# Differential attention rewritten as a pipeline over its iterations, with halved maxima and no filler matmuls

## The chip, the cores and the metric

The program runs on one core of a Trainium2 chip. A core has a matrix engine (TensorE; PE in the tables, its weight loads PEld), VectorE (DVE), ScalarE (ACT), GpSimd (POOL) and SyncE (SP), which issues the transfers. The engines run their own instruction lists and wait for each other by semaphores. The metric is device time in microseconds (us) of one execution, the median of several runs. TensorE's granted clock is given as a share of 2.4 GHz: 1.00 is full speed, 0.50 is 1.2 GHz.

## The reference, cut to what matters

The whole program is a GRU over 4 sequences of 512 steps, differential attention on its states, a spectral filter with the output projection, a second attention and a layer of experts. Only the differential attention is touched:

```
q = rotary(query @ Wq);  k = rotary(query @ Wk)      # 32 half heads of 16 numbers
v = query @ Wv                                       # 16 heads of 2 * 16
s = einsum('bthd,bshd->bhts', q, k) * scale
s = where(causal mask, s, -1e30);  a = softmax(s, axis=-1)
o1 = einsum('bhts,bshd->bthd', a, v1);  o2 = ... v2  # once for q1,k1 and once for q2,k2
attn1 - lambda_full * attn2, filtered along the sequence
```

Each head has two maps of scores (q1 k1 and q2 k2), both weigh the same v, and the difference of the results goes on.

## The kernel before, in words

`diff_attention_stage` works in 16 iterations: 4 sequences times 4 groups of 4 heads. One iteration holds 4 heads of 32 numbers on 128 partitions; each head has a block of 32 partitions, and map a of it (a = 0 or 1) uses 16 of them. All numbers are fp32 unless said otherwise. PSUM is one tensor `da_ps` of 8 banks of 512 numbers. An iteration of the kernel before has these parts, one after another on TensorE:

- Projection (`project`, L633 to L649): keys and queries, 4 matmuls of 128x512 each (L640); ScalarE copies them out (L687); a matmul that swaps the pairs of the rotary embedding (L644); VectorE and GpSimd form the rotated values `rot`; then 16 matmuls of 128x128 for v (L647). VectorE writes the keys of map 0 into `kp` and ScalarE those of map 1 (L691), each with the other map's rows as zeros. q is `rot` as it is.
- Output of the finished iteration (`output`): 4 transposes (L662) and 4 filler matmuls.
- Maximum part (L454 to L469): for each of the 4 blocks of 128 queries, the longest first, and each map, four score matmuls, one for each head (L464), 4 mask matmuls in bf16 (L468), and one VectorE reduction over the 4 heads (L544). Two sets of 4 banks take turns; a block of index i has (i+1)*128 keys.
- Maxima to rows: VectorE rounds the maxima to bf16 and keeps the rest as a second column of `spread` (L547 to L550); 8 transposes (L477) turn them into rows; ScalarE and VectorE copy these to `top` in bf16 (L520, L554). 3 filler matmuls before and 5 behind the transposes.
- Key part (L480 to L510), 8 groups (4 blocks of keys times 2 maps), each in halves of two heads: 2 score matmuls with keys on the partitions (L494), 2 bf16 matmuls that subtract the maximum (minus one times `top`, L497), 2 mask matmuls (L501); ScalarE takes the exponential of the half (L530); VectorE adds the exponentials up in `total` (L559, L563); 4 matmuls weigh v (L508), one group behind the scores.
- Sums (L514): 8 matmuls that sum `total` over the partitions. Then ScalarE forms a reciprocal by Ln and Exp, VectorE refines it (L567, L569) and scales and combines the maps (L747, L750). This runs on while TensorE projects the next iteration.

The filler matmuls (`keep_warm`, L446 to L449) multiply zeros into a free bank and nothing reads them; 12 stand in an iteration. The order of the work is written out by hand; semaphores carry the waits. SyncE loads the states `hb` and weights `wg` of the next iteration when v is done.

The second attention, `full_attention_stage` (names `fa_`, lines L930 to L1288), is not changed. It is already a pipeline over iterations: it works on the maximum part of iteration `it` and puts the projections of `it + 1` between the pieces, takes maxima in halves of two heads, and has no filler. It has no mask and a single map. Its rows are therefore of use here.

Of the kernel before, what the change touches and what calls it, by code (L numbers as in the profile page):

```python
# [407 lines left out]
class AttentionCore:  # L408
# [3 lines left out]
    def __init__(self, nc, ctx, sem, prefix, NA, scale, causal):  # L412
        self.nc, self.NA, self.scale, self.causal = nc, NA, scale, causal

        def sb(name, shape, dt=F32):
            return ctx.enter_context(nc.sbuf_tensor(prefix + name, shape, dt))

        self.probT = sb("probT", [P, 2, HG, T])
        self.mx, self.mxb = sb("mx", [P, TT, NA, HG]), sb("mxb", [P, TT, NA, HG], BF16)
        self.spread = sb("spread", [P, TT, NA, HG, DH])  # L420
        self.kp = sb("kp", [P, NA, T])
        self.negone, self.top = sb("negone", [P, P], BF16), sb("top", [P, NA, T], BF16)
        self.ones, self.rec = sb("ones", [P, P]), sb("rec", [P, NA, T])
        self.err, self.total = sb("err", [P, NA, T]), sb("total", [P, NA, HG, T])
        self.warm = sb("warm", [P, T], BF16)
        self.added, self.summed_up = sem("added"), sem("summed_up")

        self.ps = ctx.enter_context(nc.psum_tensor(prefix + "ps", [P, 8, T], F32))
        self.core_set, self.scored, self.max_done, self.spread_done = (sem(n) for n in ("core_set", "scored", "max_done", "spread_done"))
        self.max_cols, self.top_act, self.top_dve, self.rounded = sem("max_cols"), sem("top_act"), sem("top_dve"), sem("rounded")  # L430
        self.keys_scored, self.exp_done, self.refined, self.banks_free = (sem(n) for n in ("keys_scored", "exp_done", "refined", "banks_free"))
        self.product, self.ln_done, self.rec_done = sem("product"), sem("ln_done_core"), sem("rec_done")
        self.SET = 3
        self.groups = [(i, a) for i in range(TT) for a in range(NA)]

        self.queries = [(i, a) for i in reversed(range(TT)) for a in range(NA)]

    def setup(self, dve):
        nc = self.nc
        nc.vector.memset(self.warm[:], 0.0)  # L440
        nc.vector.memset(self.ones[:], 1.0).then_inc(self.core_set, 1)
        nc.vector.memset(self.negone[:], -1.0).then_inc(self.core_set, 1)
        nc.vector.memset(self.spread[:], 0.0).then_inc(self.core_set, 1)
        dve.wait_ge(self.core_set, self.SET)

    def keep_warm(self, bank, n):  # L446

        for _ in range(n):
            self.nc.tensor.matmul(self.ps[:, bank, :], self.warm[:, 0:P], self.warm[:], start=True, stop=True)  # L449

    def tensor(self, pe, it, v, q, ident, identb, mask, maskT):
        nc, NA, NG = self.nc, self.NA, len(self.groups)
        slots = [slice(DH * h, DH * h + DH) for h in range(HG)]
        for m, (i, a) in enumerate(self.queries):  # L454
            L = (i + 1) * P if self.causal else T
            bank = 4 * (m % 2)
            if m == 1:

                pe.wait_ge(self.banks_free, it * 1 + 1)
            if m >= 2:  # L460

                pe.wait_ge(self.max_done, it * NG + m - 1)
# [3 lines left out]
            if self.causal:  # L466
                for h in range(HG):
                    last = nc.tensor.matmul(self.ps[:, bank + h, i * P:L], identb, mask, start=False, stop=True)  # L468
# [1422 lines left out]
```

## Time and profile before

| | |
|---|---|
| median of 3 runs | 4769.63 us (4766.91 to 4773.21) |
| profiled execution, its own time | 4766.31 us |
| span of the profiled execution | 4764.7 us |
| TensorE busy | 3911.8 us, 82% |
| VectorE, ScalarE, GpSimd busy | 2238.0, 1304.5, 382.9 us |
| mean granted TensorE clock | 0.94 |

The span runs from the first to the last instruction; 1.6 us of the execution's time lie around it. Busy times add up the instructions of an engine. TensorE's are partly models: of matmuls that overlap, their starts are reliable and their durations overlap. An fp32 matmul shows as two records, so that four matmuls are "x8". In a timeline, the bracket behind an instruction is the idle time of the engine before it and what ended that. The differential attention runs from 2137.4 us to 3023.7 us.

### The profile page before, as it was taken

What the parts mean: (1) busy time and instruction counts of PE and PEld (TensorE: products, weight loads), DVE (VectorE), ACT (ScalarE), POOL (GpSimd) and SP (SyncE); (2) the same over time, 40 slices, a digit from 0 to 9 for tenths busy, and PEclk for the clock granted to TensorE, in tenths of its full rate; (3) what the DMA queues carried; (4) which work ended last, traced back from release to release, by engine and by line L of the source; (5) the groups of instructions that cost most, each with busy time, mean ns of one, the idle gap of its engine ahead of it and who ended that gap; (6) DMA issues with size and microseconds to landing.
All of it is one profiled execution on the core that took longest, in us unless ns stands there. A gap on an engine that the chain in (4) does not pass through costs nothing. (4 is left out here: it accounts for less than half of the span.)

```text
span 4764.7 us, 168106 instructions
## 1 busy us (share of the span) xinstructions
PE 3911.8 (82%) x69376; PEld 2562.6 (54%) x69376; DVE 2238.0 (47%) x6160; ACT 1304.5 (27%) x4110; POOL 382.9 (8%) x829
## 2 busy tenths in 40 slices
PE   8788888888888888879999999576999979488830
PEld 4377777777777777764444444333333334244410
DVE  2155555555555555545555555233666633221224
ACT  1033333333333333322223333122444411011100
POOL 0000000000000000000000000000000004300034
PEclk9999999999999999999999999788999979799975
DMA  2230000000000000000100000201111111287866
GB/s 67 48 147 0 0 0 0 0 0 0 0 0 0 0 0 0 0 22 31 46 31 31 31 31 31 74 18 42 60 62 46 46 49 67 90 258 240 256 175 157
DMA packets 144600, 256.56 MB, mean 54 GB/s; under 512 B 25943, under 2 KB 76375, under 8 KB 142516
## 3 DMA queue, kind: packets, MB, share of 16 engines
q1 hardware_dynamic: 118516, 201.96, 13.1%
q0 software_dynamic: 21248, 53.30, 4.0%
q10 hardware_dynamic: 4800, 0.81, 0.1%
q8 instruction: 23, 0.38, 0.0%
q14 instruction: 13, 0.11, 0.0%
HBM read 147.95 MB, written 62.92 MB: 44 GB/s over the span
## 5 line engine op out<-in xcount | busy, mean ns | idle before, releaser
L305 PE MATMUL gru_pr<-gru_whh,h 128*4 128x128 f32 x16384 | 544.4, 274 | 229.8 <-DVE h L396 229.8
L305 PEld LDWEIGHTS gru_pr<-gru_whh,h 128*4 128x4 f32 x16384 | 388.9, 87 | 373.3 <-DVE h L396 367.1
L305 PE MATMUL gru_pz<-gru_whh,h 128*4 128x128 f32 x16384 | 541.7, 273 | 2.3 <-issue 2.3
L305 PE MATMUL gru_pn<-gru_whh,h 128*32 128x128 f32 x16384 | 541.6, 273 | 0.0
L305 PEld LDWEIGHTS gru_pn<-gru_whh,h 128*32 128x32 f32 x16384 | 458.4, 110 | 1.3
L305 PEld LDWEIGHTS gru_pz<-gru_whh,h 128*4 128x4 f32 x16384 | 438.9, 87 | 9.9 <-issue 2.4
L376 DVE STREAM_TRANSPOSE gru_tr<-gru_pr 128x128 f32<-128x128 f32 x512 | 162.2, 317 | 379.7 <-PE gru_pr L305 379.7
L340 ACT ACTIVATE gru_rn<-gru_pre 128x16 f32<-128x16 f32 x512 | 118.5, 231 | 706.9 <-DVE gru_pre L378 706.9
L389 DVE STREAM_TRANSPOSE gru_tz<-gru_pz 128x64 f32<-128x64 f32 x1024 | 194.8, 228 | 121.3 <-PE gru_pz L305 121.3
L530 ACT ACTIVATE da_probT<-da_ps 128x1024 f32<-128x1024 f32 (+3 forms) x256 | 180.1, 703 | 195.4 <-PE da_ps L501 194.1
L280 POOL COPY gru_pick<-ident 128x4 f32 x512 | 95.9, 187 | 1687.5 <-PE gru_pz L296 1682.2
L296 PE MATMUL gru_pz<-gru_zin,gru_pick 128*4 128x128 f32 x4096 | 206.3, 273 | 19.6 <-DMA gru_whh<-in_L_cond_W_hh 19.6
L396 DVE TENSOR_TENSOR_SCAN h<-gru_d 128x32 f32<-128x32 f32 x1024 | 185.8, 223 | 77.8 <-ACT gru_d L345 76.3
L380 DVE STREAM_TRANSPOSE gru_tn<-gru_pn 128x128 f32<-128x128 f32 x512 | 162.2, 317 | 119.6 <-PE gru_pn L305 119.6
L544 DVE TENSOR_REDUCE da_mx<-da_ps 128x4 f32<-128x2048 f32 (+3 forms) x128 | 184.0, 1486 | 70.8 <-PE da_ps L468 70.5
L345 ACT ACTIVATE gru_d<-gru_tz 128x8 f32<-128x8 f32 x1024 | 177.3, 216 | 128.9 <-DVE gru_tz L389 128.9
L342 ACT ACTIVATE gru_d<-gru_narg 128x32 f32<-128x32 f32 x512 | 120.8, 236 | 329.6 <-DVE gru_narg L385 329.6
L494 PE MATMUL da_ps<-da_rot,da_kp 32*128 32x128 f32 (+3 forms) x1024 | 206.9, 480 | 0.0
L290 PE MATMUL gru_pn<-gru_bias,gru_one 128*32 128x128 f32 x4096 | 206.4, 273 | 0.0
L1620 PE MATMUL ex_pg<-ex_wg,ex_xT 128*128 128x384 f32 x512 | 192.6, 523 | 0.0
L1436 POOL DMA_INDIRECT xg<-ro_yb,ro_slot x96 | 96.4, 1004 | 1058.4 <-DVE ro_slot L1545 1030.3
L1222 DVE TENSOR_REDUCE fa_mx<-fa_ps 128x2 f32<-128x1024 f32 x128 | 150.6, 1218 | 53.8 <-PE fa_ps L1042 53.7
(270 smaller groups left out, 5521.7 us busy)
## 6 DMA issues: line engine op xcount, KB each, us to landing
ex_wg<-in_L_ffn_gate_up_proj SPq DMA_DIRECT2D x64, 768.0 KB, 5.3
ex_wd<-in_L_ffn_down_proj SPq DMA_DIRECT2D x64, 384.0 KB, 6.1
xg<-gru_zeros SPq DMA_DIRECT2D x4, 4096.0 KB
da_hb<-wide SPq DMA_DIRECT2D x16, 1024.0 KB, 4.7
fa_hb<-xnT SPq DMA_DIRECT2D x16, 1024.0 KB
ex_xg<-xg SPq DMA_DIRECT2D x64, 256.0 KB, 2.7
eo<-ex_eo POOLq DMA_DIRECT2D x64, 256.0 KB, 6.3
da_wg<-ahead SPq DMA_DIRECT2D x48, 256.0 KB, 4.8
```

The source lines that it names most:

```text
L290: nc.tensor.matmul(pn[32 * j:32 * j + 32, 0:P], one[:], bias[:, j, :], start=True, stop=False)
L296: last = nc.tensor.matmul(pz[32 * j:32 * j + B, par, 0:P], pick[:, par, :], zin[:, j * P:(j + 1) * P], start=True, stop=False)
L305: last = nc.tensor.matmul(rows(j), of(c), whh[:, c, g, j, :], start=(c == 0 and start), stop=(c == KD - 1))
L345: nc.scalar.activation(cb(d1[:, half * HS:(half + 1) * HS, 2]), tz[:, half * HC:(half + 1) * HC, 0:B], ACT.Sigmoid).then_inc(z_act, 1)
L376: nc.vector.transpose(tr[:].rearrange("p c x -> p (c x)"), pr[:, 0:P]).then_inc(tr_done, 1)
L380: nc.vector.transpose(tn[:], pn[:, 0:P]).then_inc(tn_done, 1)
L389: nc.vector.transpose(tz[:, half * HC:(half + 1) * HC, :].rearrange("p c x -> p (c x)"), pz[:, par, half * 64:(half + 1) * 64]).then_inc(t ...
L396: nc.vector.tensor_tensor_scan(t.h[:].rearrange("p c x -> p (c x)")[:, half * 64:(half + 1) * 64:2], d0[:, of, :].rearrange("p c o -> p (c ...
L494: nc.tensor.matmul(self.ps[:, h, q0:T], self.kp[slots[h], a, kt * P:(kt + 1) * P], q[slots[h], q0:T], start=True, stop=False)
L530: nc.scalar.activation(self.probT[:, n % 2, heads, q0:T], self.ps[:, heads, q0:T], ACT.Exp, scale=self.scale).then_inc(self.exp_done, 1)
L544: nc.vector.tensor_reduce(self.mx[:, i, a, :], self.ps[:, bank:bank + HG, 0:L], AX, ALU.max).then_inc(self.max_done, 1)
L1620: last = nc.tensor.matmul(pg[:, u % 2, 0:2 * I], xT[:, u % 2, k, :], wg[:, u, k, :], start=(k == 0), stop=(k == KD - 1))
```

## The change

The stage is written anew as one function; `AttentionCore` is gone. The reference's result is computed as before. What is different:

- Iteration `it` now holds the maximum part and the key part of `it`, with the projections of `it + 1` and the sums and the output of `it - 1` between the pieces. The first and the last iteration are written out apart.
- The maximum part takes 16 pieces of two heads (`score_for_max`, m = 0 to 15) in place of 8 of four heads. Pieces take banks 0, 1 and 2, 3 in turn.
- q gets a copy for each map, made by ScalarE, with the other map's rows zero. In `kp` of each map one of these unused rows holds minus one. The maxima, transposed in fp32, are added to q by VectorE (`maxima_into_q`), so that the score matmul itself subtracts the maximum. The matmuls with `top`, its two copies and the rounding to bf16 are gone.
- v passes through a second buffer `vn`, the weighed sums are copied to `pv` by ScalarE before they are scaled.
- There is no filler matmul.

```
-    def keep_warm(self, bank, n):
-        for _ in range(n):
-            self.nc.tensor.matmul(self.ps[:, bank, :], self.warm[:, 0:P], self.warm[:], start=True, stop=True)
-                    for h in heads:
-                        last = nc.tensor.matmul(self.ps[:, h, q0:T], self.negone[slots[h], :], self.top[slots[h], a, q0:T],
-                                                start=False, stop=not self.causal)
...
-        "half": np.stack([p % DH < DQ, p % DH >= DQ], 1).astype(f),
+        "half": np.stack([p % DH < DQ, p % DH >= DQ, -(p % DH == DQ).astype(f), -(p % DH == 0).astype(f)], 1).astype(f),
...
 TensorE
+    def score_for_max(it, m):
+        i, a = queries[m // 2]
+        L = (i + 1) * P
+        heads = (2 * (m % 2), 2 * (m % 2) + 1)
+        if m in (0, 2):
+            pe.wait_ge(q_ready, it * 2 + (a + 1))
+            pe.wait_ge(keys_ready, it * 2 + (a + 1))
+        if m >= 2:
+            pe.wait_ge(max_done, it * HV + (m - 1))
+        for h in heads:
+            nc.tensor.matmul(ps[:, h, 0:L], q[slots[h], a, i * P:(i + 1) * P], kp[slots[h], a, 0:L], start=True, stop=False)
+        for h in heads:
+            last = nc.tensor.matmul(ps[:, h, i * P:L], identb[:], maskb[:], start=False, stop=True)
+        last.then_inc(scored, 1)
+    def iteration(it, first=False, last=False):
+        j = it + 1
+        def maxima(m):
+            score_for_max(it, m)
+            score_for_max(it, m + 1)
+        maxima(0)
+        if not first:
+            sum_exponentials(it - 1)
+        maxima(2)
+        if not last:
+            project(j, 1, (0, 1), first)
+        maxima(4)
+        if not last:
+            project(j, 1, (2, 3))
+        maxima(6)
+        if not last:
+            project(j, 0, (0, 1), first)
+        maxima(8)
+        if not last:
+            project(j, 0, (2, 3))
+            swap_pairs(j, 1)
+        maxima(10)
+        if not first:
+            output(it - 1)
+        maxima(12)
+        maxima(14)
+        if not last:
+            swap_pairs(j, 0)
+        maxima_to_rows(it, first)
+        for n in range(NG):
+            score_keys(it, n)
+            if n < TT and not last:
+                if n == 0:
+                    pe.wait_ge(q_topped, it * 2 + 1)
+                project_v(j, n)
+            if n == 1:
+                pe.wait_ge(v_set, it * 1 + 1)
+                if not last:
+                    pe.wait_ge(sined, j * 2 + 2)
+                else:
+                    pe.wait_ge(pv_kept, it * 1)
+            if n:
+                weigh_values(it, n - 1)
+        weigh_values(it, NG - 1)
...
 ScalarE
+    def halves_of_q(j):
+        act.wait_ge(rotated, j * 2 + 3)
+        for a in range(2):
+            nc.scalar.activation(q[:, a, :], rot[:, 0, :], ACT.Copy, scale=half[:, a:a + 1]).then_inc(q_ready, 1)
+    def iteration(it, first=False, last=False):
+        j = it + 1
+        if not first:
+            move_v(it)
+            reciprocal(it - 1)
+        if not last:
+            keep_raw(j, 1)
+            keep_raw(j, 0)
+        if not first:
+            keep_output(it - 1)
+        for n in range(NG):
+            if n == 0 and not first:
+                act.wait_ge(added, it * NG)
+            exponentials(it, n)
+            if n == TT and not last:
+                keep_v(j)
+        if not last:
+            act.wait_ge(keys_scored, it * HV + HV)
+            halves_of_q(j)
+        keep_products(it, first)
...
 VectorE
+    def output(it):
+        dve.wait_ge(rec_done, it * 1 + 1)
+        nc.vector.tensor_tensor(err[:], ps[:, BSUM:BSUM + 2, :], rec[:], ALU.mult).then_inc(refined, 1)
+        dve.wait_ge(refined, it * 2 + 1)
+        nc.vector.scalar_tensor_tensor(rec[:], err[:], -2.0, rec[:], op0=ALU.add, op1=ALU.mult).then_inc(refined, 1)
+        dve.wait_ge(refined, it * 2 + 2)
+        dve.wait_ge(pv_kept, it * 1 + 1)
+        for a, o in enumerate((o1, o2)):
+            nc.vector.scalar_tensor_tensor(o[:], pv[:, a, :], -1.0, rec[:, a, :], op0=ALU.mult, op1=ALU.mult).then_inc(scaled, 1)
+        dve.wait_ge(scaled, it * 2 + 2)
+        nc.vector.scalar_tensor_tensor(aT[:], o2[:], nlam[:, 1:2], o1[:], op0=ALU.mult, op1=ALU.add).then_inc(aT_ready, 1)
+    def maxima_spread(it):
+        dve.wait_ge(max_done, it * HV + HV)
+        for a, col in enumerate((DQ, 0)):
+            nc.vector.tensor_copy(spread[:, :, a, :, col], mx[:, :, a, :]).then_inc(spread_done, 1)
+    def maxima_into_q(it):
+        for a in range(2):
+            dve.wait_ge(max_cols, it * 2 + (a + 1))
+            nc.vector.tensor_tensor(q[:, a, :], q[:, a, :], ps[:, BSUM + a, :], ALU.add).then_inc(q_topped, 1)
+    def iteration(it, first=False, last=False):
+        j = it + 1
+        for m in range(4):
+            maximum(it, m)
+        if not first:
+            output(it - 1)
+        for m in range(4, 14):
+            maximum(it, m)
+        if not last:
+            times_sine(j, 1)
+        maximum(it, 14)
+        maximum(it, 15)
+        maxima_spread(it)
+        if not last:
+            times_sine(j, 0)
+        maxima_into_q(it)
+        for n in range(NG):
+            if n == 3 and not last:
+                rotate(j, 1)
+                rotate(j, 0)
+            if n == NG - 1 and not last:
+                dve.wait_ge(keys_scored, it * HV + HV)
+                halves_of_keys(j)
+            accumulate(it, n)
```

The order of instructions on TensorE shows the interleaving. In the kernel before the loop's maximum part starts like this, each row a run of equal matmuls with L464 the scores and L468 the masks:

```order
L464 MATMUL da_ps<-da_kp,da_rot 128x512 x4
L468 MATMUL da_ps<-da_maskb,da_identb 128x128 x4
L464 MATMUL da_ps<-da_kp,da_rot 128x512 x4
L468 MATMUL da_ps<-da_maskb,da_identb 128x128 x4
L462 ISA
L464 MATMUL da_ps<-da_kp,da_rot 128x384 x4
```

In the changed kernel the same place in the loop, with L528 the scores, L530 the masks and L503 projections of the next iteration, reads:

```order
L503 MATMUL da_ps<-da_hb,da_wg 128x512 x2
L526 REGISTER_ALU
L528 MATMUL da_ps<-da_kp,da_q 128x384 x2
L530 MATMUL da_ps<-da_maskb,da_identb 128x128 x2
L526 REGISTER_ALU
L528 MATMUL da_ps<-da_kp,da_q 128x384 x2
L530 MATMUL da_ps<-da_maskb,da_identb 128x128 x2
L503 MATMUL da_ps<-da_hb,da_wg 128x512 x2
```

Two of the eight projection matmuls now stand between every two pairs of pieces, and a piece is two heads. On VectorE the last iteration, whose rows are not broken by register instructions, shows where the output of the iteration before has gone. L763 are the maxima, L767 to L775 the output, L780 `spread`, L785 the maxima into q:

```order
L763 TENSOR_REDUCE da_mx<-da_ps 128x2 x4
L767 TENSOR_TENSOR da_err<-da_ps,da_rec 128x1024
L769 SCALAR_TENSOR_TENSOR da_rec<-da_err,da_rec 128x1024
L773 SCALAR_TENSOR_TENSOR da_o<-da_pv,da_rec 128x512 x2
L775 SCALAR_TENSOR_TENSOR da_aT<-da_o,da_nlam 128x512
L763 TENSOR_REDUCE da_mx<-da_ps 128x2 x12
L780 COPY da_spread<-da_mx 128x4x4 x2
L785 TENSOR_TENSOR da_q<-da_q,da_ps 128x512 x2
```

The output, which stood behind all additions of its own iteration, is now queued behind the fourth maximum of the next, and twelve maxima are queued behind it.

## Rows read from the trace of the kernel before

**Rows 1.** Timeline of GpSimd: start, duration, engine, line; one L628 pair an iteration.
```profile
2144.07 1.26 POOL L628 TENSOR_TENSOR da_cc<-da_qk,da_cs 128x512 f32<-128x512 f32 x1 [31.36 <-ACT da_qk L687]
...
2309.64 1.48 POOL L628 TENSOR_TENSOR da_cc<-da_qk,da_cs 128x512 f32<-128x512 f32 x1 [49.75 <-ACT da_qk L687]
...
2364.09 1.48 POOL L628 TENSOR_TENSOR da_cc<-da_qk,da_cs 128x512 f32<-128x512 f32 x1 [49.75 <-ACT da_qk L687]
...
2965.03 1.48 POOL L628 TENSOR_TENSOR da_cc<-da_qk,da_cs 128x512 f32<-128x512 f32 x1 [49.75 <-ACT da_qk L687]
```
**Rows 2.** Timeline of TensorE, one iteration at full clock, parts before its maximum part.
```profile
2521.93 1.90 PE L514 MATMUL da_ps<-da_total,da_ones 128*32 128x512 f32 x16
2523.76 7.13 PE L640 MATMUL da_ps<-da_hb,da_wg 128*128 128x512 f32 x16
2530.74 1.98 PE L644 MATMUL da_ps<-da_qk,da_swap 128*128 128x512 f32 x4
2532.55 3.73 PE L647 MATMUL da_ps<-da_wg,da_hb 128*128 128x128 f32 x32
2536.12 0.60 PE L662 MATMUL da_ps<-ident,da_aT 128*128 128x128 f32 x4
```
**Rows 3.** Timeline of TensorE's weight loads, the same iteration: starts of the parts.
```profile
2537.51 0.31 PEld L464 LDWEIGHTS da_ps<-da_kp,da_rot 32*128 32x128 f32 x8 [0.42 <-issue]
...
2553.43 0.30 PEld L494 LDWEIGHTS da_ps<-da_rot,da_kp 32*128 32x128 f32 x4 [0.42 <-issue]
...
2576.28 0.24 PEld L514 LDWEIGHTS da_ps<-da_total,da_ones 128*32 128x32 f32 x8
```
**Rows 4.** Timeline of TensorE, the same iteration: halves of 512 and of 128.
```profile
2553.43 1.13 PE L494 MATMUL da_ps<-da_rot,da_kp 32*128 32x512 f32 x4
2554.40 0.38 PE L497 MATMUL da_ps<-da_top,da_negone 32*128 32x512 bf16 x2
2554.71 0.29 PE L501 MATMUL da_ps<-da_maskTb,da_identb 128*128 128x128 bf16 x2
2554.93 1.13 PE L494 MATMUL da_ps<-da_rot,da_kp 32*128 32x512 f32 x4
...
2574.21 0.49 PE L494 MATMUL da_ps<-da_rot,da_kp 32*128 32x128 f32 x4
2574.54 0.22 PE L497 MATMUL da_ps<-da_top,da_negone 32*128 32x128 bf16 x2
2574.69 0.29 PE L501 MATMUL da_ps<-da_maskTb,da_identb 128*128 128x128 bf16 x2
```
**Rows 5.** Groups by line and shape: busy, mean ns of one, idle before.
```profile
L544 DVE TENSOR_REDUCE da_mx<-da_ps 128x4 f32<-128x1024 f32 x32 | 39.1, 1221 | 2.0 <-PE da_ps L468 1.8
L544 DVE TENSOR_REDUCE da_mx<-da_ps 128x4 f32<-128x512 f32 x32 | 22.0, 687 | 6.1 <-PE da_ps L468 6.0
L735 DVE TENSOR_TENSOR da_sw<-da_ps,da_cs 128x512 f32<-128x512 f32 x32 | 21.9, 685 | 31.8 <-PE da_ps L644 31.8
L691 ACT ACTIVATE da_kp<-da_rot,da_half 128x512 f32<-128x512 f32 x16 | 11.6, 722 | 30.8 <-DVE da_rot L738 30.8
```
**Rows 6.** Timeline of TensorE in the second attention: a projection in two pieces, the output wait.
```profile
3573.45 1.98 PE L1004 MATMUL fa_ps<-fa_hb,fa_wg 128*128 128x512 f32 x4
...
3575.37 1.14 PE L1042 MATMUL fa_ps<-fa_kp,fa_q 32*128 32x512 f32 x8
...
3581.31 1.10 PE L1020 MATMUL fa_ps<-fa_sq,fa_headones 128*128 128x512 f32 x2 [1.23 <-DVE A L1242]
```
**Rows 7.** Stretches: length, busy time of PE, PEld, DVE, ACT, POOL, then granted clock.
```profile
3512.50:3517.50 5.00, 3.77 (x8) 1.51 (x5) 3.54 (x4) 1.22 (x2) 0.00 (x0) 0.67 0.00 0
...
3811.00:3829.00 18.00, 12.58 (x52) 4.18 (x56) 8.08 (x10) 4.47 (x5) 0.00 (x0) 0.53 0.00 0
```
**Rows 8.** Timeline of VectorE: the output at the stage's end.
```profile
3017.34 1.23 DVE L567 TENSOR_TENSOR da_err<-da_ps,da_rec 128x1024 f32<-128x1024 f32 x1 [3.68 <-ACT da_rec L536]
...
3021.19 0.75 DVE L750 SCALAR_TENSOR_TENSOR da_aT<-da_o,da_nlam 128x512 f32<-128x512 f32 x1
```

More of the change, by code:

```diff
@@ L658, in output, with sum_exponentials @@
+            def sum_exponentials(it):
+                for a in range(2):
+                    pe.wait_ge(added, it * NG + (NG - 1 + a))
+                    for h, sl in enumerate(slots):
+                        last = nc.tensor.matmul(ps[sl, BSUM + a, :], ones[:], total[:, a, h, :], start=True, stop=True)
+                last.then_inc(summed_up, 1)
             def output(it):
@@ L661, in output @@
                 for i in range(TT):
[L662 removed]
+                    last = nc.tensor.transpose(ps[:, BOUT, i * P:(i + 1) * P], aT[:, i * P:(i + 1) * P], t.ident[:])
                 last.then_inc(a_psum, 1)
[L664 to L673 removed]
@@ L674, in _, with maxima_to_rows @@
-            attend(NIT - 1)
+            def maxima_to_rows(it, first):
+                pe.wait_ge(spread_done, it * 2 + 2)
+                for a in range(2):
+                    if a == 1 and not first:
+                        pe.wait_ge(a_written, it * 1)
+                    for i in range(TT):
+                        last = nc.tensor.transpose(ps[:, BSUM + a, i * P:(i + 1) * P],
+                                                   spread[:, i, a, :, :].rearrange("p h d -> p (h d)"), t.ident[:])
+                    last.then_inc(max_cols, 1)
@@ L675, in _ @@
+            project(0, 1, range(KD), first=True)
+            project(0, 0, range(KD), first=True)
+            swap_pairs(0, 1)
+            swap_pairs(0, 0)
+            for tt in range(TT):
+                project_v(0, tt)
+            over_iterations(pe, iteration)
+            sum_exponentials(NIT - 1)
             output(NIT - 1)
@@ L709, in _, with exponentials @@
-            core.scalar(act, NIT - 1)
-            output(NIT - 1)
+                                     ps[:, BOUT, :].rearrange("p (i f) -> p i f", f=P), ACT.Copy).then_inc(a_written, 1)
+            def exponentials(it, n):
+                kt, a = groups[n]
+                q0 = kt * P
+                if n >= 2:
+                    act.wait_ge(product, it * NG + (n - 1))
+                    act.wait_ge(added, it * NG + (n - 1))
+                for half_of in range(2):
+                    heads = slice(2 * half_of, 2 * half_of + 2)
+                    act.wait_ge(keys_scored, it * HV + (2 * n + half_of + 1))
+                    nc.scalar.activation(probT[:, n % 2, heads, q0:T], ps[:, heads, q0:T], ACT.Exp, scale=scale).then_inc(exp_done, 1)
```

375 lines of the change are left out of this document (153 added, 222 removed).

## The prediction, made before the changed kernel ran

> **What bounds the kernel now.** I first read the slices and group table of the page to place the stage, then the timelines. GpSimd's line 628 runs twice an iteration and serves as a clock [rows 1]: the reader is to see its idle bracket repeat, 49.75 us, and to measure start to start. At full clock an iteration takes 2364.09 - 2309.64 = 54.45 us. From the first iteration's mark to the sixteenth's there are 820.96 us, 15 x 54.45 would be 816.75, so stretches at the low clock cost 4.2 us in all.
>
> The TensorE timelines cut such an iteration [rows 2, 3]; what counts is the distance between starts: sums 1.83, the two projections 6.98, two swaps 1.81, v 3.57, output and filler 1.4, from the maximum part to the key part 15.92, key part 22.85. They add up to the iteration: everything is in series on TensorE. Yet it is not all TensorE's work. In the 15.92 us it waits for VectorE's maxima and then for the turn from maxima to rows; the other parts are dense. The change can gain there, and in the matmuls that subtract the maximum, and it can lose by giving TensorE more or smaller work. So I write TensorE's list of the new iteration with prices from these rows and look for waits.
>
> **Prices.** In the key part a half of two heads has its scores, then `top`, then the mask [rows 4]. At length 512 scores take 0.97, `top` 0.31, masks 0.22; at 128 scores take 0.33 and `top` 0.15. Lengths between lie on the line (scores 0.76 and 0.54, `top` 0.25 and 0.20). A half without `top` is then 1.19, 0.98, 0.76 and 0.55 for 512, 384, 256 and 128. That two heads and their mask cost this in the new maximum part too is an assumption: the same shapes, the other operand as weights. A maximum over two heads reads half as much: 1.22 us for 1024 numbers, 0.69 for 512 [rows 5], by the same line 0.95 for 768 and 0.42 for 256.
>
> Projections are now cut in pieces of two matmuls among 32-row scores. The second attention does that: such a piece takes 1.92 us from start to start [rows 6], against 6.98 / 4 = 1.75 in one run [rows 2]. I charge 0.17 for each cut, for the four pieces of v too. The Trainium skill, "TensorEngine Tiling (Array Packing)", Tiling Modes, says that changing the tiling mode drains the engine, which speaks against cutting and halving. The trace agrees, with these 0.17 us; without a drain the eight pieces would be 1.4 us cheaper an iteration.
>
> **The new iteration, maximum part.** TensorE's work in it: pieces 4 x (1.19 + 0.98 + 0.76 + 0.55) = 13.9; sums of the iteration before 1.85; four pieces of projection 4 x 1.92 = 7.7; one swap 0.9; output 0.5. Together 24.85. Halving costs TensorE here (four heads ran side by side before, now two), but VectorE was the limit there, and the projections fill what would be idle.
>
> The wait in it: VectorE's output (L767 to L775) is 4.6 us long, as at the stage's end [rows 8], and stands behind the fourth maximum. The fourth piece ends at 2.38 + 1.85 + 2.38 = 6.6 us, its maximum at 8.0, the output at 12.6, the fifth maximum at 13.6. Behind the output on VectorE stand all later maxima, and the seventh piece needs the fifth maximum. TensorE has only a piece of projection, two pieces of maxima and another piece of projection until then: 6.6 + 1.92 + 1.96 + 1.92 = 12.4. It waits some 1.2 to 1.3 us; the second attention shows the like, 1.23 us on its output [rows 6]. The reciprocal on ScalarE is no wait: it is two activations of 1024 numbers behind the sums, about 1 us each by L691's 0.72 for 512, and ends near 6.5, before VectorE comes to it. Later VectorE catches up, since it has 0.4 to 0.7 us of work to a piece.
>
> So the last piece ends at 26.1. Behind it VectorE still has a sine product (0.69) and two maxima (0.42 each), partly begun, and is done 1.0 later; two small copies 0.35, four transposes 0.7, maxima into q of map 0, 0.69 (priced by L735, [rows 5]), hand-overs 0.1. The second swap and the second sine lie beside these. Key part at 26.1 + 2.85 = 29.0.
>
> **Key part.** It was 22.85 [rows 3]. The 16 `top` pairs go: 4 x (0.31 + 0.25 + 0.20 + 0.15) = 3.65. v comes in: 3.57 + 4 x 0.17 = 4.25. ScalarE's exponentials hide behind TensorE as before, for its halves still last longer than an exponential, and v lies between. VectorE's two rotations and two multiplies for the keys, under 1 us each as L735 is, fit: it waits between its additions for exponentials. At the end the next maxima need q of map 0, which ScalarE writes after the last exponential: 0.72 [rows 5], beside 0.3 of weighing v. That wait is 0.45. Sum 22.85 - 3.65 + 4.25 + 0.45 = 23.9.
>
> The full-clock iteration is 29.0 + 23.9 = 52.9 us, 1.6 less than before (52.85 unrounded). SyncE's loads, now released when v ends about 8 us before the iteration's end (four short groups and the end), have some 15 us until their first use, the fifth piece of the next maximum part; if that cover were gone, TensorE would wait for the rest of the transfer in every iteration.
>
> **The ends.** The first iteration lacks sums, output and their wait: 52.85 - 1.85 - 0.5 - 1.3 = 49.2, 5.25 less than an old one. Fourteen run at 52.85: 14 x 1.6 = 22.4 less. The last has no projections to put under VectorE: output done at 12.6, then twelve maxima that take turns with their pieces, about 9.1, then 1.85 to the key part, at 23.55; key part 19.2 without v and without the wait. Together 42.75 to the last sums, where before it were 15.92 + 22.85 = 38.8: 4.0 more. The start pays 1.3 (a second copy of v and a half of q in ScalarE's list before the first piece, about as long as L691's 0.72 each [rows 5]). Sum of these: -5.25 - 22.4 + 4.0 + 1.3 = -22.35.
>
> **The clock.** The profile shows full clock, 2.4 GHz, in most of the stage. In the second attention, without filler, a stretch around the output wait fell to 0.67 in the mean, that is partly to 1.2 GHz, and 18 us of the last iteration, where TensorE waited for maxima, ran at 0.53 [rows 7]. The Trainium skill, "TensorE: Matmul & The Clock Gate", Part 1, says that the throttled state is the default and that activity releases it; the trace agrees, with those 0.53. By that the filler's absence counts against the change. I take 1 for the first iteration, 5 for the middle ones (about what the 15 iterations of before lost, 4.2 [rows 1], since the waits are now shorter but fewer are filled), and 7 for the last: 18 us at 0.53 with TensorE busy 12.6 of them lose up to 6 to 7. That makes 13 in place of 4.2, 8.8 more.
>
> **Sum.** -22.35 + 8.8 = -13.5 against the profiled execution's 4766.31: 4752.8. The median of the runs shown is 3.3 above the profiled one, so 4756 us.
>
> **Bounds.** Mode changes: 1.4 us less an iteration if the cuts cost nothing, 1.5 more if each of the 16 new pieces pays 0.1 more than its half did. Output wait: 0 to 2.5 (double, if the ends of the hand-overs come late). The end of the maximum part: at best 1.85, as in the last iteration; at worst the 3.6 of before. The copies from PSUM to SBUF and back (pv, vn, v) lie on ScalarE, busy a third of the iteration: 0, and if they delayed the reciprocal they would move the output by at most 1 us. Minus one as a row of keys adds no instruction: 0, but the second `half` multiply has an added term, 0 to 0.1. Together an iteration lies between 51.2 and 54.3, that is -23 to +20 around the sum; the clock adds -7 to +20.
>
> **Rivals.**
> - *The clock falls at the output wait of every iteration.* Place: the seventh piece. For it: the second attention fell there [rows 7]. Against: it has the same wait in all its iterations and fell in few. At about 1.7 us each (a 5 us stretch at 0.67), 14 cost 24 in place of 5: 4756 + 19 = 4775, no change.
> - *Long low stretches without filler, slower.* The same place, but the clock stays low over the rest of the maximum part, some 12 us in which TensorE is now dense, so that each loses up to 6. With 10 of 14 iterations: 60 - 5 = 55 more, 4811. It decides from about 5 such iterations on. For it: 18 us in one piece in the last iteration of the second attention. Against: only where TensorE had long waits again and again, here they are 1.3, 0.5 and 0.45 in 53 us.
> - *Small pieces eat the gain.* TensorE is the bound all through, and every cost of switching shows. At 53.8 an iteration: 14 x 0.95 = 13 more, 4769, no change.
> - *Hand-overs cost less than I charge.* No output wait in excess and cheap cuts, 51.4 an iteration: 20 less, 4736.
>
> **Chances.** Forecast 0.50 (its own range 4743 to 4768), clock at every wait 0.14, long low stretches 0.12, small pieces 0.11, cheap hand-overs 0.13. A measurement tells 0.2% of this kernel from no change, which is 9.5 us: below 4760 is faster, above 4779 slower. Faster: four fifths of the forecast's 0.50, the 0.13 and 0.02 of the others, 0.55. Slower: 0.12 and 0.03 of the others, 0.15. Same: 0.30. The range that leaves out two tenths: 4732 to 4784.
>
> **What would show it.** In the new profile: GpSimd's mark near 52.9 us apart at full clock; the seventh piece waiting about 1.3 us for a maximum behind VectorE's output; 2.4 to 3.4 us between the last piece and the key part, partly filled by a swap; key part near 23.9 to the next piece, with 0.45 of it a wait for ScalarE's q; the last iteration's maximum part near 23.5, at a clock near 0.5 for much of it. Wrong it is if pieces of two heads take more than 1.3 us at 512, if projection pieces take more than 2, if VectorE is late at other pieces, or if low stretches stand in most iterations.

## The result, and the profile after

The kernel became slower: 4807.5 us in the median (4795.6 to 4819.5, 7 runs) against 4769.6 us (4762.4 to 4787.6, 7 runs), a ratio of 1.0078 with an interval of 1.0059 to 1.0098. The forecast was 4756 us, with a range up to 4784: the sign was wrong and the time lies outside the range. The profiled execution took 4803.15 us (span 4801.5). The page shows more TensorE time in fewer matmul records (68,672 instead of 69,376), and a lower clock above all in the 26th of its 40 slices, which holds the end of the stage (5 tenths, 7 before):

```profile
PE 3973.3 (83%) x68672; PEld 2565.5 (53%) x68672; DVE 2265.1 (47%) x6302; ACT 1324.4 (28%) x4142; POOL 379.3 (8%) x829
...
PEclk9999999999999999999999999588999989799965
```

I measure the stage from the start of its first projection to the end of its last sums, both on TensorE's timeline: 877.8 us before, 909.1 after, so 31.4 of the 37 us are there. GpSimd's mark (first of each pair, L489 now) answers to [rows 1]:

```profile
2166.84 1.26 POOL L489 TENSOR_TENSOR da_cc<-da_qk,da_cs 128x512 f32<-128x512 f32 x1 [21.76 <-ACT da_qk L647]
...
2385.63 1.26 POOL L489 TENSOR_TENSOR da_cc<-da_qk,da_cs 128x512 f32<-128x512 f32 x1 [44.27 <-ACT da_qk L647]
...
2439.56 1.26 POOL L489 TENSOR_TENSOR da_cc<-da_qk,da_cs 128x512 f32<-128x512 f32 x1 [44.27 <-ACT da_qk L647]
...
2495.22 1.26 POOL L489 TENSOR_TENSOR da_cc<-da_qk,da_cs 128x512 f32<-128x512 f32 x1 [44.31 <-ACT da_qk L647]
...
2931.62 1.26 POOL L489 TENSOR_TENSOR da_cc<-da_qk,da_cs 128x512 f32<-128x512 f32 x1 [44.27 <-ACT da_qk L647]
```

From the second row to the third it is 53.93 us, an iteration at full clock (54.45 before, 52.85 forecast). To the fourth it is 55.66: 6 of the 14 middle iterations are so long. All fourteen take 764.8 us. TensorE's timeline shows the cause (line, shape of weights and data, then the wait ahead):

```profile
2435.88 0.92 PE L528 MATMUL da_ps<-da_kp,da_q 32*128 32x384 f32 x4
2436.73 0.28 PE L530 MATMUL da_ps<-da_maskb,da_identb 128*128 128x128 bf16 x2
2436.85 1.94 PE L503 MATMUL da_ps<-da_hb,da_wg 128*128 128x512 f32 x4
2439.80 0.92 PE L528 MATMUL da_ps<-da_kp,da_q 32*128 32x384 f32 x4 [1.02 <-DVE da_mx L763]
2440.87 0.91 PE L528 MATMUL da_ps<-da_kp,da_q 32*128 32x384 f32 x4
2441.72 0.39 PE L530 MATMUL da_ps<-da_maskb,da_identb 128*128 128x128 bf16 x2
2441.89 3.57 PE L503 MATMUL da_ps<-da_hb,da_wg 128*128 128x512 f32 x4
```

The seventh piece waits 1.02 us for VectorE, which is busy with the output. Right behind that wait the projection piece takes 3.57 us instead of 1.94: half clock, 1.65 us lost. The last iteration is far worse. It takes 68.0 us from its first piece (2972.07) to its last sums (3040.07), where the old one took 38.9 and the forecast said 49.75. The clock falls near 2981.1, inside the sixth piece, while TensorE is at work: the scores take 1.05 us instead of 0.92 and the mask behind them 0.39 instead of 0.29. The wait of 4.00 us for the seventh piece comes behind that:

```profile
2979.14 0.91 PE L528 MATMUL da_ps<-da_kp,da_q 32*128 32x384 f32 x4
2979.98 0.29 PE L530 MATMUL da_ps<-da_maskb,da_identb 128*128 128x128 bf16 x2
2980.41 1.05 PE L528 MATMUL da_ps<-da_kp,da_q 32*128 32x384 f32 x4
2981.39 0.39 PE L530 MATMUL da_ps<-da_maskb,da_identb 128*128 128x128 bf16 x2
2985.79 1.65 PE L528 MATMUL da_ps<-da_kp,da_q 32*128 32x384 f32 x4 [4.00 <-DVE da_mx L763]
```

In the stretches (length, busy time of PE, PEld, DVE, ACT, POOL, granted clock, DMA) it doesn't come back before the last sums, though from the start of the key part (3003.37) on TensorE is busy without a gap:

```profile
2975.00:2980.00 5.00, 4.96 (x33) 1.40 (x26) 3.04 (x3) 2.08 (x2) 0.00 (x0) 1.00 0.02 3
...
3010.00:3040.00 30.00, 30.00 (x146) 10.13 (x148) 8.69 (x8) 9.21 (x14) 0.00 (x0) 0.50 0.00 1
```

The kernel before went through the same iteration at full clock, though TensorE was idle for a quarter of its maximum part and nothing full-width but the short masks stood between its pieces. Its own projections and v stood right ahead of them, and its pieces held four heads. It entered its key part high, with filler of 3 and 5 matmuls (L449) around the turn, which the change takes out:

```profile
2974.00:2989.00 15.00, 10.96 (x108) 5.33 (x107) 11.89 (x11) 0.69 (x2) 0.00 (x0) 1.00 0.01 1
2989.00:3013.00 24.00, 23.88 (x194) 9.49 (x192) 9.83 (x9) 11.73 (x17) 0.00 (x0) 1.00 0.00 1
```

### The profile page after: what moved, and what is told of

Its sections match the earlier page's. It is cut to its first block and busy times, and to the rows that moved or that the text cites. A ratio compares the mean times of both kernels' runs of the same rounds, so it can differ in the third digit from the quotient of the medians.

```text
span 4801.5 us, 166900 instructions
## 1 busy us (share of the span) xinstructions
PE 3973.3 (83%) x68672; PEld 2565.5 (53%) x68672; DVE 2265.1 (47%) x6302; ACT 1324.4 (28%) x4142; POOL 379.3 (8%) x829
## 5 line engine op out<-in xcount | busy, mean ns | idle before, releaser
L763 DVE TENSOR_REDUCE da_mx<-da_ps 128x2 f32<-128x1024 f32 (+3 forms) x256 | 208.2, 823 | 160.2 <-PE da_ps L530 157.4
L528 PE MATMUL da_ps<-da_kp,da_q 32*128 32x128 f32 (+3 forms) x1024 | 215.5, 498 | 23.4 <-DVE da_mx L763 18.3
L566 PE MATMUL da_ps<-da_q,da_kp 32*128 32x128 f32 (+3 forms) x1024 | 217.3, 502 | 5.4 <-DVE da_q L785 5.4
```

Source lines behind the costliest of these rows:

```text
L528: nc.tensor.matmul(ps[:, h, 0:L], q[slots[h], a, i * P:(i + 1) * P], kp[slots[h], a, 0:L], start=True, stop=False)
L566: nc.tensor.matmul(ps[:, h, q0:T], kp[slots[h], a, kt * P:(kt + 1) * P], q[slots[h], a, q0:T], start=True, stop=False)
L763: nc.vector.tensor_reduce(mx[:, i, a, banks], ps[:, banks, 0:(i + 1) * P], AX, ALU.max).then_inc(max_done, 1)
```

## The experiments

All start from the changed kernel. "Stage" is measured as above, "last" from the last iteration's first piece to its last sums, both in the profiled execution. A clean iteration is the shortest of the fourteen middle ones; it is at full clock in all runs but e6_nomask, where every one of them has a low stretch. The ratio is to the kernel before on the same chip; a run of one execution has none. The stages can be compared from chip to chip: the changed kernel's took 909.1 us on one and 909.5 on another.

| run | clean iteration | last | stage | ratio (interval) |
|---|---|---|---|---|
| before | 54.45 | 38.9 | 877.8 | 1 |
| after | 53.93 | 68.0 | 909.1 | 1.0078 (1.0059 to 1.0098) |
| e12_after_again | 53.93 | 68.0 | 909.5 | 1.0088 (1.0066 to 1.011) |
| e1_last_fill | 53.93 | 66.4 | 907.9 | 1.0061 (1.0035 to 1.0086) |
| e4_split_out | 52.84 | 65.9 | 881.5 | 1.0011 (0.9993 to 1.0029) |
| e5_pairs | 52.55 | 66.4 | 900.0 | one execution |
| e6_nomask | 53.57 | 61.5 | 897.1 | one execution |
| e7_pairs_split | 52.05 | 64.3 | 867.9 | 0.9993 (0.9965 to 1.002) |
| e8_dense_last | 53.93 | 54.7 | 894.4 | one execution |
| e2_key_fill | 53.93 | 56.1 | 893.5 | one execution |
| e9_top_last | 55.01 | 58.6 | 908.7 | one execution |
| e10_split_fill | 52.84 | 47.7 | 861.5 | 0.9984 (0.9964 to 1.0004) |
| e11_all | 52.05 | 47.4 | 852.5 | 0.9969 (0.9953 to 0.9986) |

**e1_last_fill: filler once in the last iteration.**

```
+                if last:
+                    pe.wait_ge(pv_kept, it * 1)
+                    keep_warm(5, 18)      # behind the sixth piece; matmuls of 128x512 bf16 on zeros
```

> The changed kernel with 18 filler matmuls (128x512, bf16, zeros) in the last iteration alone, behind its sixth piece, where TensorE waited 4.0 us for the seventh maximum. The last iteration, first piece to last sums, took 68.0 us in the changed kernel. My theory: that one wait brought the clock down to 1.2 GHz and the thin pieces of two heads behind it did not bring it back; with the wait filled the last iteration takes 43 to 47 us and the kernel about 22 less than the changed one (4785). Rival: the last iteration falls by itself, because no full-width matmuls of projections stand in it; then the clock falls later in it and it still takes 55 to 68 us. A second rival, that the filler only delays: 68 or more.

The clock had fallen inside the sixth piece here too, 0.9 us ahead of the filler. The filler covered the wait and brought the clock back up, and it stayed up for 4 us of thin pieces behind it. Then it fell, with no wait near (the fall is inside a piece at 2996.3), and stayed down:

```profile
2991.80:2996.80 5.00, 4.86 (x30) 1.99 (x28) 2.99 (x4) 0.00 (x0) 0.00 (x0) 0.97 0.00 0
2996.80:3001.80 5.00, 5.00 (x28) 2.74 (x24) 2.06 (x4) 0.60 (x1) 0.00 (x0) 0.50 0.00 0
...
3006.80:3040.00 33.20, 33.20 (x133) 10.09 (x132) 9.14 (x8) 10.49 (x14) 0.00 (x0) 0.50 0.00 1
```

The last iteration gained 1.6 us and took 66.4, within the 55 to 68 of the first rival. My theory of that moment, that the one wait is what costs, fell; covering it is not enough.

**e4_split_out: VectorE's output in two stretches.**

```
-                for m in range(4, 14):
+                for m in range(4, 6):
                     maximum(it, m)
+                if not first:
+                    output_rest(it - 1)   # the two o and aT; err and rec stay behind the fourth maximum
+                for m in range(6, 14):
+                    maximum(it, m)
```

> The changed kernel with VectorE's output cut in two: the two refining operations stay behind the fourth maximum, the three that scale and combine stand behind the sixth. Theory: the wait of 1.02 us before the seventh piece goes in each of the 14 middle iterations, and with it the fall of the clock that stood behind it in 6 of 14 (1.65 us each): an iteration at full clock takes 52.9 in place of 53.93, mean 53.0 in place of 54.63, the kernel about 22 less (4785). Rival: the wait only moves to the ninth piece or to the end of the maximum part, where VectorE is late by as much; the iteration stays at 53.9.

Confirmed for the middle iterations. The seventh piece no longer waits and the next projection piece (2330.53) runs at full clock:

```profile
2326.64 1.94 PE L503 MATMUL da_ps<-da_hb,da_wg 128*128 128x512 f32 x4
2328.50 0.91 PE L528 MATMUL da_ps<-da_kp,da_q 32*128 32x384 f32 x4
2329.35 0.28 PE L530 MATMUL da_ps<-da_maskb,da_identb 128*128 128x128 bf16 x2
2329.56 0.92 PE L528 MATMUL da_ps<-da_kp,da_q 32*128 32x384 f32 x4
```

All fourteen iterations take 52.8 to 52.9 us. That is 1.09 us less each, the wait itself, and no 1.65 for the clock in any. So in the middle iterations the wait was what lowered the clock; why it did so in only 6 of 14 was not tested. The stage is 27.6 us shorter, nearly all that the change had lost. The last iteration is nearly as bad as ever, 65.9 us: the wait in it came down to 2.13 us, and the clock fell all the same, 0.1 us behind its end.

**e5_pairs and e6_nomask: is it the pieces of two heads?** The first puts the scores of four heads ahead of their masks, still in two signals (the edit below is shortened); the second has no masks there.

```
-                for h in heads:                                     # e5: four heads, then their masks
+                for half_of in range(2):
+                    if m >= 2: pe.wait_ge(max_done, it * HV + (m + half_of - 1))
+                    for h in (2 * half_of, 2 * half_of + 1): scores
+                for half_of in range(2): masks of its two heads, then_inc(scored, 1)
```

> The changed kernel with the two pieces of one query block and map issued together: scores of all four heads, then the masks of both halves, each half still signalled apart. Theory: a piece of two heads pays for two of four row groups and for one change to the full array and back, so the pair at 512 falls from 2.55 us to about 1.4 and TensorE's work in the maximum part falls by some 8 us; but the scores of a pair now wait for both maxima before, and the wait behind VectorE's output grows to about 3 us, so the iteration at full clock is 53.0 to 53.6 and the clock falls there more often. Rival: the price of halving is small, the pair takes over 2 us, and the longer waits make the iteration 55 or more.

> The changed kernel without the 32 mask matmuls of the maximum part; the maxima then run over all keys up to the block's end, later ones too. Theory: the full-array masks between 32-row scores are what keeps two pieces from running side by side; without them two pieces at 512 take 1.1 to 1.3 us from the first's start to the end of issue of the second in place of 2.55, and VectorE bounds the maximum part: iteration about 49 us. Rival: only the masks' own 0.22 us go, two pieces take 2.1, the iteration 50.5 to 51.

Four heads with masks take 1.40 us at length 512 (two pieces took 2.55), without masks 1.07. TensorE does become shorter, but VectorE does not, and the wait grows by what TensorE saved: 2.36 us in e5_pairs, 3.51 in e6_nomask, and the projection behind it is at half clock in 11 of 14 middle iterations of the one and in all 14 of the other:

```profile
2335.99 1.78 PE L528 MATMUL da_ps<-da_kp,da_q 32*128 32x384 f32 x8 [2.36 <-DVE da_mx L763]
2337.70 0.40 PE L531 MATMUL da_ps<-da_maskb,da_identb 128*128 128x128 bf16 x4
2337.93 3.62 PE L503 MATMUL da_ps<-da_hb,da_wg 128*128 128x512 f32 x4
```

```profile
2434.74 2.52 PE L528 MATMUL da_ps<-da_kp,da_q 32*128 32x384 f32 x8 [3.51 <-DVE da_mx L761]
2437.18 3.78 PE L503 MATMUL da_ps<-da_hb,da_wg 128*128 128x512 f32 x4
```

Cheaper pieces alone are worth little, 9.1 us of the stage in e5_pairs: VectorE's output is the limit there. Both expectations had the price of a pair right and the iteration wrong: 52.55 instead of 53.0 to 53.6 us in e5_pairs, with more low clock, and 53.6 to 55 instead of 49 in e6_nomask.

**e7_pairs_split: both.** The edits of e5_pairs and e4_split_out together.

> The scores of four heads and then their masks, in two signals (as in e5_pairs), together with VectorE's output in two stretches (as in e4_split_out). Theory: a piece of four heads then costs 0.1 us or more less than two pieces, and with the split no wait stands before the seventh piece, so the clock doesn't fall: a clean iteration of about 50.5 to 51.5 us against 52.85 in e4_split_out and 53.93 of the changed kernel; fourteen iterations give 28 to 30 us less than e4_split_out, so about 0.995 of the kernel before. The last iteration stays at half clock, about 65 us. Rival: TensorE isn't the bound of the maximum part once its pieces are short, VectorE's maxima are; then the waits come at other pieces, the clock falls there, and an iteration stays at 52.5 to 54 us.

The stage gains another 13.6 us on e4_split_out, but the fourteen middle iterations only 6.3 of the 28 to 30 that I expected of them; 4.8 come from the first iteration and 1.6 from the last. Clean iterations take 52.05 us, and 5 of the 14 take 52.9 to 53.2 because the clock dips. The rival holds for the missing part: the seventh piece still waits 0.24 us for VectorE's maxima, and four later ones 0.78, 0.16, 0.23 and 0.40.

**e8_dense_last: full-width filler between all pieces of the last iteration.**

```
+                if last: keep_warm(5, 8)     # in place of each projection piece: 8, 8, 8 and 12
+                if last: keep_warm(5, 4)     # in place of the swap before maxima_to_rows
+                    if n < TT and last: keep_warm(BV, 4)   # in place of each v piece
```

> The changed kernel, with 8, 8, 8, 12 and 4 filler matmuls of 128x512 bf16 on zeros in the last iteration where the other iterations have their projections and transposes, and 4 at each place of a v piece; their results are read by nobody. Theory: what holds the clock in the other iterations is the full-width work that stands between the thin pieces; with it the last iteration runs at full clock for nearly all of its length and takes 52 to 55 us from its first piece to its last sums, filler included, against 68.0 us without. Rival: the clock falls at the first wait of 4 us for the output of the iteration before and stays low whatever stands between; then 75 us or more.

Confirmed: 54.7 us, one dip, and back to full clock behind it, where in the changed kernel it never came back:

```profile
2975.00:2988.00 13.00, 12.01 (x68) 4.00 (x64) 10.10 (x11) 3.48 (x4) 0.00 (x0) 1.00 0.00 1
2988.00:2993.00 5.00, 4.88 (x18) 1.79 (x19) 2.85 (x4) 0.00 (x0) 0.00 (x0) 0.67 0.00 0
2993.00:3010.00 17.00, 16.66 (x103) 7.93 (x103) 7.23 (x13) 2.94 (x4) 0.00 (x0) 1.00 0.01 1
```

Some 13 us of useless matmuls made the iteration 13 us shorter. They also fill most of the wait, of which 1.11 us are left; that the wait isn't the cause rests on e1_last_fill and on where the clock falls.

**e2_key_fill and e9_top_last: does the key part need `top` to hold the clock?**

```
+                    keep_warm(5, 16)         # both: last iteration, ahead of the key part
+                    if last:                 # e9: between scores and masks
+                        for h in heads:
+                            nc.tensor.matmul(ps[:, h, q0:T], warm[slots[h], 0:P], warm[slots[h], q0:T], start=False, stop=False)
```

> The changed kernel with 16 filler matmuls of 128x512 ahead of the key part of the last iteration, and nothing else. Theory: the clock rises to 2.4 GHz with the filler and falls back to half in the midst of the key part, as it did after the filler of e1_last_fill, so that from the end of the filler to the last sums there are 28 us or more. Rival: entered at full clock, the key part holds it, as in the kernel before, and takes 21 to 24 us.

> The changed kernel, in the last iteration alone: 16 filler matmuls ahead of the key part, and in the key part a bf16 matmul of 32 rows of zeros for each head between its scores and its mask, as the row of the maximum stood there in the kernel before. Theory: the kernel before kept full clock through its last key part because its three thin matmuls to a head kept TensorE busier; the key part then stays at 2.4 GHz after the filler and takes 21 to 24 us. Rival: the two kernels differ there only by the state in which they enter the key part; then e9_top_last and e2_key_fill do the same, whichever that is.

The rival of both holds. Entered at full clock, the key part keeps it without `top`; it takes 20.8 us (3009.87 to 3030.71) instead of 36.7 in the changed kernel. With `top` it takes 22.9 and keeps it too. In e2_key_fill:

```profile
2985.00:3005.00 20.00, 15.88 (x69) 8.06 (x70) 10.68 (x18) 0.60 (x1) 0.00 (x0) 0.50 0.00 0
3005.00:3010.00 5.00, 5.00 (x23) 2.44 (x23) 1.38 (x2) 0.00 (x0) 0.00 (x0) 0.81 0.00 0
3010.00:3030.00 20.00, 20.00 (x148) 7.53 (x152) 9.12 (x7) 10.87 (x15) 0.00 (x0) 1.00 0.01 2
```

So the same list of matmuls, without a gap, takes 36.7 us at 1.2 GHz or 20.8 us at 2.4 GHz, by the level at which it was entered. The other runs bear this out. The last key part was entered low and took 36.7 us in the changed kernel, e12_after_again, e1_last_fill, e4_split_out, e5_pairs, e6_nomask and e7_pairs_split; it was entered high and took 20.8 in e2_key_fill, e10_split_fill and e11_all. The kernel before entered it high.

e9_top_last also differed from its expectation, by a name used twice in the code: in all other iterations the second half of each key group got the added matmuls as well. That prices `top` in the new key part, side by side (halves without, then with it):

```profile
2406.52 1.13 PE L571 MATMUL da_ps<-da_q,da_kp 32*128 32x512 f32 x4 [0.39 <-DVE da_q L797]
2407.58 0.28 PE L577 MATMUL da_ps<-da_maskTb,da_identb 128*128 128x128 bf16 x2
2407.80 1.13 PE L571 MATMUL da_ps<-da_q,da_kp 32*128 32x512 f32 x4
2408.76 0.38 PE L575 MATMUL da_ps<-da_warm 32*128 32x512 bf16 x2
2409.07 0.28 PE L577 MATMUL da_ps<-da_maskTb,da_identb 128*128 128x128 bf16 x2
2409.19 1.11 PE L518 MATMUL da_ps<-da_wg,da_hb 128*128 128x128 f32 x8
```

With `top` the masks start 1.27 us after the scores, without it 1.06. Scores to `top`, both of 32 rows, take 0.96; scores to the full-array mask take 1.06. A removed `top` at 512 thus gives 0.21 us, not the 0.31 from its start to the mask's in [rows 4]. The middle iterations agree: eight halves with it cost 55.01 - 53.93 = 1.08 us, 0.135 each, where my prices of 0.31, 0.25, 0.20 and 0.15 have a mean of 0.23. So does the last key part, where all 16 halves have it: 22.9 - 20.8 = 2.1 us.

**e10_split_fill, e11_all and e12_after_again: what it comes to.** e10 is e4_split_out and e11 is e7_pairs_split, each with filler of 8 matmuls at the four places of the last iteration's projections and 4 ahead of its turn; e12 is the changed kernel again.

```
+                if last: keep_warm(5, 8)     # four times, from behind the fourth piece on
+                if last: keep_warm(5, 4)     # before maxima_to_rows; none in the key part
```

> VectorE's output in two stretches (as in e4_split_out) and filler in the last iteration's maximum part alone, 8 matmuls of 128x512 bf16 at each of the four places where the others have a projection piece and 4 ahead of the turn of the maxima. Theory: the fourteen iterations stay at 52.85 us, the filler holds the clock through the maximum part, and the key part, entered at full clock, holds it by itself (as in e2_key_fill): the last iteration then takes 46 to 48 us (52.85 less 13.7 of projections, swaps and v, plus 36 times 0.24 of filler) instead of 65.9 in e4_split_out, and the kernel goes from 1.0011 to about 0.997 of the kernel before. Rival: the clock falls at one of VectorE's waits in the maximum part in spite of the filler, as in one window of e8_dense_last, and with no full-width work in the key part it doesn't come back: 58 us or more.

> e7_pairs_split with the filler of e10_split_fill: four heads to a piece, the output in two stretches, filler in the last iteration's maximum part. Theory: iterations of 52.1 to 52.9 us as in e7_pairs_split, a last iteration of 45 to 48 us instead of 65, so about 0.9955 of the kernel before, faster than both kernels. Rival: with pieces of four heads TensorE waits for VectorE's maxima longer in the last iteration, the clock falls between the fillers and the last iteration takes over 55 us; then about 0.998.

> The changed kernel itself, unchanged, on the chip of these runs. Theory: what e4_split_out and e7_pairs_split gained was gained against it, so it stands at 1.006 to 1.010 of the kernel before here too, with iterations of 53.93 and 55.6 us and a last one of 66 to 68 us. Rival: chips differ in how far the clock falls; then the ratio here is another, and the differences between runs of different calls can't be read as gains.

All three came as the theory said, the ratios of e10_split_fill and e11_all 0.0014 higher than forecast. In e10_split_fill the last iteration takes 47.7 us and both its parts run at full clock:

```profile
2957.00:2982.00 25.00, 24.84 (x150) 10.59 (x152) 17.39 (x23) 3.91 (x5) 0.00 (x0) 1.00 0.00 1
2982.00:3004.00 22.00, 21.54 (x171) 8.56 (x173) 10.76 (x10) 11.27 (x16) 0.00 (x0) 1.00 0.01 1
```

e11_all beats both kernels: 0.9969 of the kernel before (0.9953 to 0.9986), and 1.2% less than the changed kernel on the same chip, 4791.7 us against 4850.6. Besides dips in the first and in five of the middle iterations, it has one in the last, 0.76 for 7 us ahead of the key part, at waits of 0.23 and 0.40 us:

```profile
2940.00:2958.00 18.00, 17.49 (x110) 7.04 (x108) 13.77 (x15) 3.31 (x4) 0.00 (x0) 1.00 0.00 1
2958.00:2965.00 7.00, 6.04 (x45) 4.25 (x43) 3.06 (x8) 0.60 (x1) 0.00 (x0) 0.76 0.01 2
2965.00:2986.00 21.00, 20.66 (x156) 7.90 (x154) 10.40 (x9) 10.97 (x16) 0.00 (x0) 1.00 0.00 1
```

## Why the prediction was wrong, step by step

The terms of the forecast and what the profile after has in their place:

| term | forecast | measured | miss |
|---|---|---|---|
| start, first projection to first piece, more than before | +1.3 | +0.8 | -0.5 |
| first iteration | 49.2 + 1 | 56.6 | +6.4 |
| fourteen middle ones, full clock | 14 x 52.85 | 14 x 53.93 | +15.1 |
| their low clock | 5 | 10.0 | +5.0 |
| last iteration | 42.75 + 7 | 68.0 | +18.3 |

The misses add up to 44.3 us, and the forecast of -13.5 for the stage became +31.4. The 0.6 us between the two are small terms, among them the last sums, 3.10 us long instead of 1.90.

- **The step that failed most: the clock of the last iteration.** I let the clock be low only where TensorE waits, "18 us at 0.53", and took the key part at full clock. It fell 0.7 us ahead of the output wait, inside a piece, and stayed at 1.2 GHz for 59 us, to the last sums. The maximum part took 31.3 us instead of 23.55 and the key part 36.7 instead of 19.2; the key part alone lost 36.7 - 20.8 = 15.9 us by the clock. Where the clock falls is not bound to the wait: in e12_after_again, the same kernel, it fell inside the wait, 11 us behind the first piece instead of 9, and in e5_pairs and e7_pairs_split ahead of it, 8.5 and 8.6 us behind the first piece, with pieces of four heads and waits of 1.20 and 0.22 us before it. e8_dense_last and e10_split_fill show that full-width matmuls among the thin pieces of the maximum part hold the clock or bring it back; the other iterations have them as projections. e2_key_fill shows that the key part needs none in it if it is entered high. e1_last_fill shows that it isn't the wait alone. [Rows 7] held the warning, for there the clock was at 0.53 with TensorE busy 70% of the time; I read busy time as what raises the clock. The Trainium skill, "TensorE: Matmul & The Clock Gate", Part 1, has activity release the throttled state; with e8_dense_last the trace agrees, where filler brought the clock back; in the changed kernel's last key part it doesn't, for TensorE was busy 30.00 us of 30.00 and the clock stayed at 1.2 GHz.
- **The mode change, in the key part: mis-sized.** Key part and end were to take 23.9 us and took 24.93. `top` gives back 0.1 less in each half than its start-to-start distance, since the step to the full-array mask is then paid behind the scores. Its price was in the range (0.1 for each of 16), not in the sum. The same rule of the Trainium skill that I used for the cuts, "TensorEngine Tiling (Array Packing)", Tiling Modes, says that changing the mode drains the engine. I applied it to the projections, where it was nearly right, and forgot that removing `top` removes no change.
- **The maximum part: right by luck, as misses cancelled.** First piece to key part 29.0 forecast, 29.0 measured. Pieces of two heads take 1.28, 1.07, 0.85 and 0.64 where I had 1.19, 0.98, 0.76 and 0.55 (before a full-width piece, 0.97 at 384, as priced). The projection piece at 1.87 instead of 1.92, the wait at 1.02 instead of 1.2 to 1.3, and 2.5 from the last piece to the key part instead of 2.85 made up for it. A half of two heads costs as much as four heads did: scores 1.13 us for x4 here, 1.14 for x8 in e5_pairs.
- **The output wait: place, cause and length right.** That is the one that I could have removed: e4_split_out gets 1.09 us an iteration from it.
- **The clock at that wait.** Rival 1 had the place and the price (1.7 us each, measured 1.65) but said every iteration; 6 of 14 fell. Rival 2, slower with 4811, had nearly the right time by another place: no middle iteration stayed low, the last one did. Rival 3 had 53.8 us for an iteration, near the 53.93 measured, but by costs of switching all through; most of the excess lies in the key part, by `top`. The first iteration was at half clock for its second to fourth pieces and the projection behind them, shortly behind a wait of 1.96 us for q, and again around its turn; by the same pieces at full clock that cost 4.8 and 1.1 us. A run on that alone wasn't made.
- **The end wait** was 0.18 to 0.22 us instead of 0.45, and the profile puts it down to VectorE's keys (`da_kp`, L756), not to ScalarE's q: the engine was forecast wrong. The v pieces took 1.04 us, 1.06 forecast.
- **Outside the stage.** The profiled execution is 36.8 us longer, the stage 31.4. The code behind the stage is the same; from the last sums to the span's end it took 1745 to 1801 us in the thirteen profiled executions, and 8.8 us more after than before. e11_all's stage is 25.3 us shorter than before's, its time by the ratio only 15 (7 to 23). What the remaining difference comes from stays open.

Slower, to which I gave 0.15 (0.12 by rival 2), happened, and the reasons for it in the forecast were only a part of the cause.

## What to carry to other kernels

In an iteration without its usual dense matmuls (the last of a pipeline, above all), don't ask only whether TensorE is busy: look for a stretch of the same thin shapes in the trace, read its clock and the level at which it was entered, and price it at both levels. If it may be entered low and nothing full-width stands in it, take the lower one. When an instruction between two others goes, price what its neighbours then cost side by side. And where TensorE waits for a long list on another engine, split that list before making TensorE's work cheaper: here the split gave 27.6 us of the stage, the cheaper pieces without it 9.1 and a longer wait.

## What the runs showed of the hardware that I had not expected

- The level of the clock is held, not only earned: one list of 32-row fp32 matmuls with 128x128 masks and 128x32 products, busy without a gap, took 36.7 us at 0.50 and 20.8 us at 1.00, by the level at which it began.
- The clock can fall while TensorE works: in the last iteration it went to 0.50 inside a piece, 9 us behind the first piece, with gaps of no more than 0.2 us before.
- Behind 17 recorded filler matmuls the clock was high for 4 us of thin pieces and then fell with no wait in them (e1_last_fill); behind 16 ahead of the key part it stayed high for more than 20 us (e2_key_fill). What makes the thin pieces of the maximum part lose it and those of the key part keep it was not separated; the key part has products of 128 rows between its halves.
- Two heads of 32 rows take as long as four: 1.13 and 1.14 us at length 512. Behind 32-row scores a full-array mask starts 0.1 us later than a 32-row `top` does (1.06 and 0.96 us).
